# Splitting the third VectorE operation off an activation chain and queueing it one step later, in an eight-core transformer layer

## The chip, the cores and the metric

The kernel runs on the 8 cores of one Trainium2 chip. Each core computes two of the sixteen sequences on its own; nothing is exchanged between cores. The metric is the device time of the slowest core in microseconds (us). Engines are named as in the profile: PE (TensorE), ACT (ScalarE), DVE (VectorE), POOL (GpSimd), SP (SyncE).

## The reference

One pre-norm transformer layer on x of shape 16 x 2048 x 1024, with 16 heads and a feed-forward width of 4096:

```python
x = x + attention(layernorm(x), w_qkv, b_qkv, w_proj, b_proj)
x = x + ffn(layernorm(x), w1, b1, w2, b2)

# ffn: round to multiples of 1/256, piecewise-linear GELU with 33 breakpoints on [-4, 4]
h = float2fix(einsum('bsd,df->bsf', x, w1) + b1, 8)
h = pwlin_gelu_basic(h, 8, 8)       # interp of the exact GELU, 0 below -4, identity above 4
h = float2fix(h, 8)
out = float2fix(einsum('bsf,fd->bsd', h, w2) + b2, 8)
```

## The kernel before

Each engine has a program of its own. The builder walks once through the work and appends closures to one list, each for one engine; an engine executes its own closures in the order in which they were appended. Between engines there are only counting semaphores: `c_v` counts what DVE has finished, `c_s` ACT, `c_pe` PE. `wait_ge(c_v.sem, w)` holds the issuing engine, and all that is queued behind on it, until DVE has counted to `w`.

The first part (layer norm, QKV, attention, projection) writes the intermediate x1s to DRAM. The second part is the feed-forward network, and the change lies in it. It has 8 blocks of 512 tokens (two sequences, four blocks each). A block has 32 groups (`hm`) of 128 hidden channels, and a group is one tile of 128 channels by 512 tokens. The groups of all blocks are numbered through as `h` (0 to 255). A main loop runs over steps `g` (0 to 258). A step appends pieces of four groups, in this order:

- `act_E012(g)`: PE multiplies the eight slices of w1 by xn2 into one of two PSUM halves (L956; the half comes free when ACT has read the group two before); ACT reads it into `ft` (L970, "E1"); DVE clamps and rounds (L981, L984).
- `act_E34(g-1)`: ACT scales into `fu5` (L996); DVE rounds and subtracts (L1004, L1006).
- `act_E56(g-2)`: ACT adds a half (L1022) and takes two GELUs, into `fgl` (L1023) and `fji` (L1025); DVE subtracts them (L1034), multiplies by `fu5` into `fki` (L1036), and adds `fgl` into `fu5` (L1039), with an explicit drain between each two.
- `act_E78(g-3)`: ACT adds the rounding constant (L1055) and writes the finished tile to `gbuf` (L1057). Before L1055 it waits for DVE's L1039 of that group, which was queued one step earlier.

So in a step ACT executes L970, L996, L1022, L1023, L1025, L1055, L1057, and DVE executes L981, L984, L1004, L1006, L1034, L1036, L1039.

Other work is interleaved by `hm`. At `hm` 3, 6, ..., 24 the step begins with 32 matmuls of the second product for the block before (`w2_mm`, L1089); the first of them waits for the last `gbuf` tile of the block before, which L1057 writes at `hm` 2. At `hm` 5, 8, ..., 26 the DVE part of the step begins with three operations that evacuate such a product (`w2_ev`, L1113, L1118, L1120). At `hm` 5, 9, 13, 17 the layer norm of the next block puts, after L981 and L984, two statistics operations and two small ones on DVE, and ACT waits for them before a square root with its table load (`ln2_A`, L862 to L876). At `hm` 6, 10, 14, 18 DVE takes a reciprocal and a product, and ACT waits for them before it normalises a tile (`ln2_B`, L887, L889, L901). After the last step eight `w2_mm` with `w2_ev` follow.

Of the kernel before, what the change touches and what calls it, by code (L numbers as in the profile page):

```python
# [10 lines left out]
ALU = mybir.AluOpType  # L11
# [38 lines left out]
def build():  # L50
# [15 lines left out]
    p = Prog()  # L66
    with es:
# [26 lines left out]
        c_v = Ctr(es, nc, "c_v")  # L94
# [26 lines left out]
        def ev(g):  # L121
            g.dma_start(out=identb[:], in_=ident).then_inc(c_lc.sem, 16)
            g.dma_start(out=bqt[:], in_=bqkv[0:2048].rearrange("(c q) -> q c", q=128),
                        allow_slow_non_contiguous=True).then_inc(c_lc.sem, 16)
            g.dma_start(out=b1t[:], in_=b1.rearrange("(c q) -> q c", q=128),
                        allow_slow_non_contiguous=True).then_inc(c_lc.sem, 16)
            g.dma_start(out=bvbc[:], in_=bqkv[2048:3072].partition_broadcast(128)).then_inc(c_lc.sem, 16)
            g.dma_start(out=bpbc[:], in_=bproj.partition_broadcast(128)).then_inc(c_lc.sem, 16)
            g.dma_start(out=b2bc[:], in_=b2.partition_broadcast(128)).then_inc(c_lc.sem, 16)
# [166 lines left out]
        for s in range(NSEQ):  # L296
# [125 lines left out]
            for g_ in range(4):  # L422
                for mq in range(4):
                    mc = g_ * 4 + mq
                    for tb in range(4):
                        bi = gi % 4
# [35 lines left out]
            for g_ in range(4, 6):  # L462
                nb = g_ - 4
                for tt in range(NTT):
                    bi = gi % 4
# [468 lines left out]
        e1_hist = {}  # L934
        e5_hist = {}
        e6_hist = {}
        e8_hist = {}

        def act_E012(h):
# [50 lines left out]
        def act_E34(h):  # L990
            i = h % 3
            i4 = h % 4

            def ev(sc, i=i, i4=i4, w=e1_hist[(h, "va")]):
                sc.wait_ge(c_v.sem, w)
                sc.activation(fu5[:, i, :], ft[:, i4, :], AF.Identity,  # L996
                              bias=p155[:, 0:1], scale=1.0 / 64.0).then_inc(c_s.sem, 1)
            p.on("scalar", ev)
            c_s.n += 1
            u5_done = c_s.n  # L1000

            def ev(v, i=i, i4=i4, w=u5_done):
                v.wait_ge(c_s.sem, w)
                v.tensor_scalar(fki[:, i4, :], fu5[:, i, :], MC, -MC, ALU.add, ALU.add)  # L1004
                v.drain()  # L1005
                v.scalar_tensor_tensor(ft[:, i4, :], fki[:, i4, :], -1.0, fu5[:, i, :],  # L1006
                                       ALU.mult, ALU.add).then_inc(c_v.sem, 1)
            p.on("vector", ev)
            c_v.n += 1
            e1_hist[(h, "vb")] = c_v.n  # L1010

        def act_E56(h):
            i = h % 3
            i4 = h % 4
            j = h % 2

            def ev(sc, i=i, i4=i4, j=j, w=e1_hist[(h, "vb")], fg=e6_hist.get(h - 2)):
                sc.wait_ge(c_v.sem, w)
                if fg is not None:
                    sc.wait_ge(c_v.sem, fg)  # L1020
                sc.drain()  # L1021
                sc.add(fu5[:, i, :], ft[:, i4, :], phf[:, 0:1])  # L1022
                sc.activation(fgl[:, j, :], fki[:, i4, :], AF.Gelu, bias=neg4[:, 0:1],  # L1023
                              scale=0.25)
                sc.activation(fji[:, j, :], fki[:, i4, :], AF.Gelu, bias=neg375[:, 0:1],  # L1025
                              scale=0.25).then_inc(c_s.sem, 1)
            p.on("scalar", ev)
            c_s.n += 1
            e5_hist[h] = c_s.n
            s3_done = c_s.n  # L1030

            def ev(v, i=i, i4=i4, j=j, w=s3_done):
                v.wait_ge(c_s.sem, w)
                v.tensor_sub(ft[:, i4, :], fji[:, j, :], fgl[:, j, :])  # L1034
                v.drain()  # L1035
                v.scalar_tensor_tensor(fki[:, i4, :], ft[:, i4, :], 256.0, fu5[:, i, :],  # L1036
                                       ALU.mult, ALU.mult)
                v.drain()
                v.scalar_tensor_tensor(fu5[:, i, :], fgl[:, j, :], 256.0, fki[:, i4, :],  # L1039
                                       ALU.mult, ALU.add).then_inc(c_v.sem, 1)  # L1040
            p.on("vector", ev)
            c_v.n += 1
            e6_hist[h] = c_v.n

        def act_E78(h):
            bi, hm = divmod(h, 32)
            i = h % 3
            j = h % 2

            def ev(sc, bi=bi, hm=hm, i=i, j=j, w=e6_hist[h],  # L1050
                   gg=w2_last_of.get(bi - 2)):
                sc.wait_ge(c_v.sem, w)
                if gg is not None:
                    sc.wait_ge(c_pe.sem, gg)
                sc.add(fji[:, j, :], fu5[:, i, :], cmc[:, 0:1])  # L1055
                sc.drain()  # L1056
                sc.activation(gbuf[:, bi % 2, hm, :], fji[:, j, :], AF.Identity,  # L1057
                              bias=nmc256[:, 0:1],
                              scale=1.0 / 256.0).then_inc(c_s.sem, 1)
            p.on("scalar", ev)  # L1060
            c_s.n += 1
            e8_hist[h] = c_s.n
# [3 lines left out]
        def w2_mm(bi, j):  # L1066
            s, tb = blocks[bi]
            tt, nb = j // 2, j % 2
            ob = j % 2
            par = tt % 2  # L1070
            if nb == 0:
                def ev(sy, s=s, tb=tb, tt=tt, par=par, g=x2rd_guard.get(par)):
                    if g is not None:
                        sy.wait_ge(c_v.sem, g)
                    sy.dma_start(out=x1rd2[:, par, :],
                                 in_=x1s[s, tb * TB + tt * 128:tb * TB + (tt + 1) * 128, :]
                                 ).then_inc(s_x[2 + par].sem, 16)
                p.on("sync", ev)
                s_x[2 + par].n += 16

            def ev(t, bi=bi, tt=tt, nb=nb, ob=ob, gd=g_done_of[bi],
                   g=w2ev_guard.get(ob), fw=first_w2[0]):
                if fw:
                    t.wait_ge(c_lb.sem, ldw_B)
                t.wait_ge(c_s.sem, gd)
                if g is not None:
                    t.wait_ge(c_v.sem, g)
                for hm in range(NHM):
                    ins = t.matmul(pA[:, 1024 + ob * 512:1024 + (ob + 1) * 512],  # L1089
                                   gbuf[:, bi % 2, hm, tt * 128:(tt + 1) * 128],  # L1090
                                   w2b[:, hm, nb * 512:(nb + 1) * 512],
                                   start=(hm == 0), stop=(hm == NHM - 1))
                ins.then_inc(c_pe.sem, 1)
            p.on("tensor", ev)
            c_pe.n += 1
            first_w2[0] = False
            w2_pe_of[(bi, j)] = c_pe.n
            w2_last_of[bi] = c_pe.n
# [50 lines left out]
        for g in range(NG + 3):  # L1149
            if g < NG:  # L1150
                bi, hm = divmod(g, NHM)
                if bi > 0 and hm in w2mm_marks:
                    w2_mm(bi - 1, w2mm_marks.index(hm))
                if bi > 0 and hm in w2ev_marks:
                    w2_ev(bi - 1, w2ev_marks.index(hm))
                if hm % 2 == 0 and 2 <= hm // 2 + 1 <= 15:
                    w1_group_load(bi, hm // 2 + 1)
                if hm == 30 and bi + 1 < NB:
                    w1_group_load(bi + 1, 0)
                act_E012(g)  # L1160
                if hm == 31 and bi + 1 < NB:
                    w1_group_load(bi + 1, 1)
                if bi + 1 < NB and 3 <= hm <= 20:
                    tt, st = divmod(hm - 3, 4)
                    if st == 0 and hm >= 3 and tt < 4:
                        ln2_L(bi + 1, tt)
                    elif st == 2:
                        ln2_A(bi + 1, tt)
                    elif st == 3:
                        ln2_B(bi + 1, tt)  # L1170
                    elif st == 1 and tt >= 1:
                        ln2_C1(bi + 1, tt - 1)
                        xn2_ready[bi + 1] = ln2_C2(bi + 1, tt - 1)
            if g >= 1 and g - 1 < NG:
                act_E34(g - 1)
            if g >= 2 and g - 2 < NG:
                act_E56(g - 2)
            if g >= 3 and g - 3 < NG:
                act_E78(g - 3)
                if (g - 3) % NHM == NHM - 1:  # L1180
                    g_done_of[(g - 3) // NHM] = c_s.n
# [58 lines left out]
```

## Time and profile before

| | us |
|---|---|
| time before, median of 2 runs | 3963.19 |
| the two runs | 3918.98 and 4007.39 |
| the profiled execution | 3937.67 |
| its span on the slowest core (core 6) | 3936.1 |
| its spans over the eight cores | 3896.8 to 3936.1 |
| busy of the span: PE, ACT, DVE, POOL | 2680.5, 2506.3, 1969.5, 663.3 |

The span is the time from the first to the last instruction of the core. Busy shares are means over two very different parts: the feed-forward loop begins at about 2296 us and ends at about 3874 us of the span. All rows are of core 6.

### The profile page before, as it was taken

The numbers are of one execution on the slowest core, as the hardware profiler recorded it, in microseconds if no ns is written. First come the engines' busy times: TensorE is split into PE (matmuls) and PEld (weight loads), VectorE is DVE, ScalarE is ACT, GpSimd is POOL, SyncE is SP. The second block draws the span as 40 slices with busy tenths as digits, with TensorE's granted clock in tenths as the row PEclk, the third lists the DMA queues.
The fourth block names the chain that finished last, engine by engine and source line by source line (L and its number), as shares of the span: only waits on it lengthen the run. The fifth ranks groups of instructions, "written<-read, shape, count | busy, mean of one in ns | idle before, by whom it ended". The sixth has DMA issues, their size and how long they took to land.

```text
span 3936.1 us, 41130 instructions; the slowest of 8 cores (3896.8 to 3936.1 us)
## 1 busy us (share of the span) xinstructions
PE 2680.5 (68%) x10880; PEld 939.2 (24%) x10880; DVE 1969.5 (50%) x2865; ACT 2506.3 (64%) x3102; POOL 663.3 (17%) x1234
## 2 busy tenths in 40 slices
PE   0894767677777987776768335676667666766686
PEld 0341211121213421211211111222222222322232
DVE  2013433434341134343434247676777777676794
ACT  0321857767581267585848158787878777787893
POOL 1000000000001100000000223333332333242340
PEclk9986888989898998898989667788878888888898
DMA  8322011010103200101010564344444444354451
GB/s 180 74 28 91 30 41 40 20 44 4 45 4 76 33 2 4 45 4 45 4 44 4 108 96 65 54 78 73 73 72 71 67 78 69 69 80 71 67 90 50
DMA packets 206879, 215.91 MB, mean 55 GB/s; under 512 B 24000, under 2 KB 167360, under 8 KB 206656
## 3 DMA queue, kind: packets, MB, share of 16 engines
q0 software_dynamic: 169792, 95.82, 19.9%
q1 hardware_dynamic: 36864, 117.46, 9.1%
q8 instruction: 99, 1.62, 0.2%
q14 instruction: 124, 1.02, 0.1%
HBM read 265.90 MB, written 33.55 MB: 76 GB/s over the span
## 4 chain that ended last, share of the span: by engine, by line
PE 31%; ACT 19%; DVEq 12%; DVE 11%; ACTq 10%; issue 8%; DMA 7%; POOL 1%; SPq 0%; POOLq 0%
ACT PTb L646 12%; PE pA L442 6%; PE pAT L660 6%; DMA xstream<-x 5%; PE pA L633 5%; ACTq L1056 5%; ACTq L1021 4%; PE pBT L662 4%; DVEq L983 3%; PE pA L479 3%; PE pA L1089 3%; DVE fki L1036 3%; DVEq L1035 3%; ACT fji L1025 2%; DVEq L1005 2%
## 5 line engine op out<-in xcount | busy, mean ns | idle before, releaser
L646 ACT ACTIVATE PTb<-pA,negB 128x1024 bf16<-128x1024 f32 x1024 | 1104.7, 1112 | 460.8 <-PE pA L636 439.2
L956 PE MATMUL pA<-xn,w1s 128*128 128x512 bf16 x2048 | 620.1, 463 | 450.9 <-ACT ft L970 428.1
L819 POOL DMA_DIRECT2D w1s<-w x1024 | 552.6, 585 | 1046.0 <-PE pA L956 1020.9
L660 PE MATMUL pAT<-PTb,vtm 128*65 128x512 bf16 x1024 | 410.3, 401 | 263.7 <-ACT PTb L646 191.5
L1089 PE MATMUL pA<-w2b,gbuf 128*128 128x512 bf16 x2048 | 476.3, 393 | 91.6 <-ACT gbuf L1057 91.6
L633 PE MATMUL pA<-qfm,kfm 64*128 64x512 bf16 x1024 | 406.4, 406 | 42.8 <-DVEq L734 41.5
L956 PEld LDWEIGHTS pA<-xn,w1s 128*128 128x128 bf16 x2048 | 217.0, 111 | 820.5 <-issue 674.9
L662 PE MATMUL pBT<-PTb,vtm 128*65 128x512 bf16 x1024 | 410.1, 401 | 0.0
L636 PE MATMUL pA<-qfm,kfm 64*128 64x512 bf16 x1024 | 406.7, 406 | 0.0
L602 POOL DMA_DIRECT2D attn<-stgB x64 | 33.5, 523 | 1735.6 <-PE pBT L662 1152.6
L1089 PEld LDWEIGHTS pA<-w2b,gbuf 128*128 128x128 bf16 x2048 | 207.5, 102 | 360.0 <-issue 143.0
L442 PE MATMUL pA<-xnfm,wstr 128*128 128x512 bf16 x1024 | 244.7, 407 | 8.8 <-DVEq L734 8.8
L660 PEld LDWEIGHTS pAT<-PTb,vtm 128*65 128x65 bf16 x1024 | 112.6, 110 | 574.2 <-issue 574.2
L518 DVE COPY uAB<-pAT 65x512 f32<-65x512 f32 x64 | 44.0, 687 | 409.2 <-PE pBT L662 409.2
L1034 DVE TENSOR_TENSOR ft<-fji,fgl 128x512 f32<-128x512 f32 x256 | 176.3, 689 | 117.6 <-ACT fji L1025 117.1
L970 ACT ACTIVATE ft<-pA,b 128x512 f32<-128x512 f32 x256 | 171.1, 668 | 100.6 <-PE pA L956 100.6
L530 DVE RECIPROCAL rbsb<-uAB 1x512 bf16<-1x512 f32 x64 | 214.0, 3344 | 11.3 <-issue 9.3
L538 DVE RECIPROCAL rbsb<-uAB 1x512 bf16<-1x512 f32 x64 | 210.2, 3285 | 0.0
L492 DVE TENSOR_TENSOR vtm<-pA,bvbc 128x512 bf16<-128x512 f32 x64 | 44.4, 694 | 323.6 <-PE pA L479 323.6
L633 PEld LDWEIGHTS pA<-qfm,kfm 64*128 64x128 bf16 x1024 | 91.0, 93 | 470.9 <-issue 469.6
L1022 ACT ACTIVATE fu<-ft,phf 128x512 f32<-128x512 f32 x256 | 184.9, 722 | 23.7 <-DVE ft L1006 2.6
L1057 ACT ACTIVATE gbuf<-fji,nmc 128x512 bf16<-128x512 f32 x256 | 184.8, 722 | 18.4 <-issue 1.0
(79 smaller groups left out, 3269.9 us busy)
## 6 DMA issues: line engine op xcount, KB each, us to landing
w1s<-w POOLq DMA_DIRECT2D x1024, 64.0 KB, 2.7
xstream<-x SPq DMA_DIRECT2D x96, 512.0 KB, 4.0
x1rd<-x1s SPq DMA_DIRECT2D x64, 512.0 KB, 4.5
x1s<-x1t SPq DMA_DIRECT2D x32, 512.0 KB, 2.9
out<-outt SPq DMA_DIRECT2D x64, 256.0 KB, 2.3
wstr<-wqkv POOLq DMA_DIRECT2D x96, 128.0 KB, 6.1
w2b<-w POOLq DMA_DIRECT2D x32, 256.0 KB, 26.7
attn<-stgB POOLq DMA_DIRECT2D x64, 64.0 KB, 1.9
```

What stands on the lines that cost most here:

```text
L442: ins = t.matmul(psl[bi], wstr[:, g_ % 2, dc, mq * 128:(mq + 1) * 128], xnfm[:, dc, tb * 512:(tb + 1) * 512], start=(dc == 0), stop=(dc == ...
L530: v.reciprocal(rbsb[64:65, 0:512], uAB[64:65, 0, :]).then_inc(c_v.sem, 1)
L538: v.reciprocal(rbsb[64:65, 512:1024], uAB[64:65, 1, :]).then_inc(c_v.sem, 1)
L633: t.matmul(pA[:, off:off + 512], kfm[0:64, pr, ko:ko + 128], qfm[0:64, pr, qs:qs + 512], start=True, stop=True, skip_group_check=True)
L636: t.matmul(pA[:, off + 512:off + 1024], kfm[64:128, pr, ko:ko + 128], qfm[64:128, pr, qs:qs + 512], start=True, stop=True, skip_group_chec ...
L646: sc.activation(PT[:, kt % 2, :], pA[:, off:off + 1024], AF.Exp, bias=negB[:, 0:1], scale=SCALE).then_inc(c_s.sem, 1)
L660: t.matmul(pAT[0:65, :], lhs[:, 2 * pr, :], PT[:, kt % 2, 0:512], start=(kt == 0), stop=(kt == NKT - 1), skip_group_check=True)
L662: t.matmul(pBT[0:65, :], lhs[:, 2 * pr + 1, :], PT[:, kt % 2, 512:1024], start=(kt == 0), stop=(kt == NKT - 1), skip_group_check=True).the ...
L819: gp.dma_start(out=w1s[:, sl, dc, :], in_=w1[dc * 128:(dc + 1) * 128, grp * 256:(grp + 1) * 256]).then_inc(c_lw[sl].sem, 16)
L956: ins = t.matmul(pA[:, hb * 512:(hb + 1) * 512], w1s[:, sl, dc, (hm % 2) * 128:(hm % 2 + 1) * 128], xn2[:, bi % 2, dc, :], start=(dc == 0) ...
L1056: sc.drain()
L1089: ins = t.matmul(pA[:, 1024 + ob * 512:1024 + (ob + 1) * 512], gbuf[:, bi % 2, hm, tt * 128:(tt + 1) * 128], w2b[:, hm, nb * 512:(nb + 1) ...
```

## The change

The DVE closure of `act_E56` is cut after its second operation, which now counts `c_v`. The third operation becomes a function of its own, `act_E6b(h)`, called one step later, between `act_E56(g-2)` and `act_E78(g-3)`. `act_E78` now waits for the count of `act_E6b`. The explicit drain that stood before the third operation is gone; in its place stands a wait on `c_v` for the second operation. ACT's L996 gets a further wait, for `act_E6b` three groups before. The two waits on `e6_hist` (before L970 and before L1022) keep their names and now refer to the second operation.

```diff
@@ act_E34 @@
-            def ev(sc, i=i, i4=i4, w=e1_hist[(h, "va")]):
+            def ev(sc, i=i, i4=i4, w=e1_hist[(h, "va")], vd=e6b_hist.get(h - 3)):
                 sc.wait_ge(c_v.sem, w)
+                if vd is not None:
+                    sc.wait_ge(c_v.sem, vd)
@@ act_E56 @@
                 v.scalar_tensor_tensor(fki[:, i4, :], ft[:, i4, :], 256.0, fu5[:, i, :],
-                                       ALU.mult, ALU.mult)
-                v.drain()
+                                       ALU.mult, ALU.mult).then_inc(c_v.sem, 1)
+            p.on("vector", ev)
+            c_v.n += 1
+            e6_hist[h] = c_v.n
+
+        def act_E6b(h):
+            i = h % 3
+            i4 = h % 4
+            j = h % 2
+
+            def ev(v, i=i, i4=i4, j=j, w=e6_hist[h]):
+                v.wait_ge(c_v.sem, w)
                 v.scalar_tensor_tensor(fu5[:, i, :], fgl[:, j, :], 256.0, fki[:, i4, :],
                                        ALU.mult, ALU.add).then_inc(c_v.sem, 1)
             p.on("vector", ev)
             c_v.n += 1
-            e6_hist[h] = c_v.n
+            e6b_hist[h] = c_v.n
@@ act_E78 @@
-            def ev(sc, bi=bi, hm=hm, i=i, j=j, w=e6_hist[h],
+            def ev(sc, bi=bi, hm=hm, i=i, j=j, w=e6b_hist[h],
@@ main loop @@
             if g >= 2 and g - 2 < NG:
                 act_E56(g - 2)
             if g >= 3 and g - 3 < NG:
+                act_E6b(g - 3)
                 act_E78(g - 3)
```

## Rows read from the trace of the kernel before

**Rows 1.** The page, part 1: busy us, share of the span, instructions.
```profile
PE 2680.5 (68%) x10880; PEld 939.2 (24%) x10880; DVE 1969.5 (50%) x2865; ACT 2506.3 (64%) x3102; POOL 663.3 (17%) x1234
```

**Rows 2.** Windows: before the feed-forward loop, the loop, and behind it.
```profile
core 6: us, PE busy (x) PEld busy (x) DVE busy (x) ACT busy (x) POOL busy (x), PEclk, DMA share, GB/s
...
2296.00:3874.00 1578.00, 1036.44 (x4048) 415.18 (x4046) 1159.63 (x2155) 1262.87 (x1904) 543.81 (x1008) 0.81 0.45 71
```

**Rows 3.** Waits from 2300 to 3900 us: total, times, longest.
```profile
ACT L876 <- DVE ln2d L867: 130.4, 28, 5.3
...
ACT ft L970 <- PE pA L956: 76.6, 8, 11.0
...
ACT xn2tm L901 <- DVE ln2d L889: 60.6, 28, 3.6
...
ACT fu L1022 <- DVE ft L1006: 2.6, 8, 0.5
ACT fji L1055 <- DVE fu L1039: 1.9, 3, 1.1
```

**Rows 4.** Timeline, ACT, one step: start us, duration us, operation.
```profile
2891.07 0.71 ACT L1025 ACTIVATE fji<-fki,neg 128x512 f32<-128x512 f32 x1
2891.68 0.71 ACT L1055 ACTIVATE fji<-fu,cmc 128x512 f32<-128x512 f32 x1
...
2893.09 0.67 ACT L970 ACTIVATE ft<-pA,b 128x512 f32<-128x512 f32 x1
...
2895.69 0.71 ACT L1025 ACTIVATE fji<-fki,neg 128x512 f32<-128x512 f32 x1
```

**Rows 5.** Timeline, DVE, the same step.
```profile
2891.88 0.69 DVE L1034 TENSOR_TENSOR ft<-fji,fgl 128x512 f32<-128x512 f32 x1 [0.45 <-ACT fji L1025]
2892.65 0.69 DVE L1036 SCALAR_TENSOR_TENSOR fki<-ft,fu 128x512 f32<-128x512 f32 x1
2893.41 0.69 DVE L1039 SCALAR_TENSOR_TENSOR fu<-fgl,fki 128x512 f32<-128x512 f32 x1
2894.02 0.42 DVE L981 TENSOR_SCALAR fki<-ft 128x512 f32<-128x512 f32 x1
...
2894.86 0.42 DVE L1004 TENSOR_SCALAR fki<-fu 128x512 f32<-128x512 f32 x1
2895.36 0.69 DVE L1006 SCALAR_TENSOR_TENSOR ft<-fki,fu 128x512 f32<-128x512 f32 x1
```

**Rows 6.** Timeline, both engines, the last step of the loop.
```profile
3869.69 0.71 ACT L1025 ACTIVATE fji<-fki,neg 128x512 f32<-128x512 f32 x1
...
3872.03 0.69 DVE L1039 SCALAR_TENSOR_TENSOR fu<-fgl,fki 128x512 f32<-128x512 f32 x1
3872.87 0.72 ACT L1055 ACTIVATE fji<-fu,cmc 128x512 f32<-128x512 f32 x1 [1.08 <-DVE fu L1039]
```

**Rows 7.** Timeline: ACT and DVE where E1 ended a long wait (`hm` 3).
```profile
2908.68 0.69 ACT L970 ACTIVATE ft<-pA,b 128x512 f32<-128x512 f32 x1 [10.89 <-PE pA L956]
...
2909.55 0.43 DVE L981 TENSOR_SCALAR fki<-ft 128x512 f32<-128x512 f32 x1 [10.82 <-ACT ft L970]
```

**Rows 8.** Timeline, layer-norm steps `hm` 6 and 9: DVE's L981, ACT's release.
```profile
2931.29 0.42 DVE L981 TENSOR_SCALAR fki<-ft 128x512 f32<-128x512 f32 x1
...
2932.77 1.24 ACT L901 ACTIVATE xn2tm<-x1rd,ln2d 128x1024 bf16<-128x1024 f32 x1 [1.75 <-DVE ln2d L889]
...
2950.06 0.42 DVE L981 TENSOR_SCALAR fki<-ft 128x512 f32<-128x512 f32 x1
...
2952.82 1.28 ACT L876 ACT_TABLE_LOAD   x1 [4.95 <-DVE ln2d L867]
```

**Rows 9.** Timeline, PE: matmuls of both products.
```profile
2898.05 8.76 PE L1089 MATMUL pA<-w2b,gbuf 128*128 128x512 bf16 x32 [9.94 <-ACT gbuf L1057]
...
3020.52 3.57 PE L956 MATMUL pA<-xn,w1s 128*128 128x512 bf16 x8 [6.96 <-ACT ft L970]
...
3056.65 1.89 PE L956 MATMUL pA<-xn,w1s 128*128 128x512 bf16 x8 [3.43 <-ACT ft L970]
```

More of the change, by code:

```diff
@@ L936, in build @@
         e6_hist = {}
+        e6b_hist = {}
         e8_hist = {}
```

## The prediction, made before the changed kernel ran

> **What bounds the kernel now.** The page's busy shares come first: ACT is busy for 64% of the span [rows 1]. This is a mean over unlike parts, so the windows come next. The feed-forward loop, in which the whole change lies, takes 1578 us, and in it ACT is busy for 1262.9 us, DVE for 1159.6 us and PE for 1036.4 us, with PE's granted clock at 0.81 of full speed, between its two levels of 1.2 and 2.4 GHz [rows 2]. What stands before and behind the loop is the same code in both kernels.
>
> The timeline of one step then shows how the two elementwise engines stand to each other. ACT goes from one L1025 to the next in 2895.69 - 2891.07 = 4.62 us and is never idle in it [rows 4]. DVE runs the same group one step behind and has 0.45 us to spare in the step [rows 5]. The important thing to see is that L1055 starts 0.61 us after L1025 [rows 4], while DVE has only just begun L1034 [rows 5]: ACT doesn't look at this step's DVE work, because L1055 waits for an L1039 that was queued a step before. That one step of slack is why the waits list has only 1.9 us, in 3 places, for ACT's L1055 on DVE's L1039 [rows 3]. The real waits of ACT in the loop are the layer norm's (130.4 us at L876, 60.6 us at L901) and PE at the block starts (76.6 us at L970) [rows 3]. So ACT sets the pace of ordinary steps, and DVE that of the layer-norm steps.
>
> **The change part by part.**
>
> *The moved operation and the wait for it.* In step g, DVE's queue now reads L981 and L984 of group g, L1004 and L1006 of g-1, L1034 and L1036 of g-2, and only then the third operation of g-3. Its own inputs have long been there. But it stands behind L1034 of g-2, which needs L1025 of g-2, which ACT executes directly before L1055 of g-3. And L1055 now waits for the third operation. The slack of a step is gone: in every step ACT must stand still from the end of its second GELU until DVE has done three operations.
>
> How long that is, counted from the start of L1025: L1034 starts 2891.88 - 2891.07 = 0.81 us later; L1036 0.77 us after that [rows 4, 5]; the third operation, which has no drain ahead of it any more, 0.61 us after that, as L981 follows L1039 without a drain (2894.02 - 2893.41) [rows 5]. It starts at 2.19 us. From the start of such an operation to a waiting L1055 the last step of the loop shows 3872.87 - 3872.03 = 0.84 us [rows 6]. So L1055 starts 3.03 us after L1025. The same last step is the case in small: there ACT had no slack, and L1055 started 3872.87 - 3869.69 = 3.18 us after L1025, with the drain still in it [rows 6]. Before, the distance was 0.61 us [rows 4]. An ordinary step becomes 3.03 - 0.61 = 2.42 us longer, 7.04 us for 4.62.
>
> Queued behind the waiting L1055 on ACT are L1057, then L970 of the next group, for which PE (its PSUM half) and DVE (L981) wait in turn.
>
> *How many.* There are 256 groups. For 255 the price is 2.42 us: 617.1 us. For the last one the operation has been queued right behind the one of the group before, and is done by the time ACT gets there; in place of 3.18 - 0.61 = 2.57 us ACT spends there the 1.40 us of L1055 and L1057 (L1055 to L970 is 2893.09 - 2891.68 = 1.41 us [rows 4]): -1.2 us.
>
> *What is given back.* In a layer-norm step ACT waits behind L970 for a DVE chain. Now DVE is no longer behind when L970 ends, so this wait shrinks. L981 starts 2909.55 - 2908.68 = 0.87 us after the start of an L970 that it waited for [rows 7], that is 0.20 us after its end (0.67 us long [rows 4]). From L981 the table load of L876 starts 2952.82 - 2950.06 = 2.76 us later, and L901 2932.77 - 2931.29 = 1.48 us later [rows 8]. New waits: 0.20 + 2.76 = 2.96 us and 0.20 + 1.48 = 1.68 us. The 28 old ones of each kind sum to 130.4 and 60.6 us [rows 3]; given back are 130.4 - 28 x 2.96 = 47.5 us and 60.6 - 28 x 1.68 = 13.6 us. The evacuation of a second product at the head of a step, 1.9 us of DVE (an estimate from three spacings like those of [rows 5]: 0.77, 0.50 and 0.61 us), then falls into the 2.5 us in which DVE waits for the next L970 (from 2.80 to 5.31 us after L1025: 3.03 + 1.41 + 0.87), and costs nothing. The small waits for a lagging DVE go too: 2.6 us at L1022 and 1.9 - 1.1 us at L1055 [rows 3], 3.4 us together.
>
> *What stays.* The block-start wait of 10.89 us [rows 7] runs from L1057 at `hm` 2 through 32 second-product matmuls and 8 first-product ones to L970. Both ends move together, so none of it is given back. PE elsewhere stays hidden: between two marks it has three groups and one second product, at most 3 x 3.57 + 8.76 = 19.5 us [rows 9], against three steps of 21.1 us. DVE's own step: L1004 comes 0.84 us after L981 [rows 5], L1006 0.50 us after that and lasts 0.69 us [rows 5], so it ends by 5.31 + 0.84 + 0.50 + 0.69 = 7.34 us, before the next L1034 is released at 7.04 + 0.81 = 7.85 us, and DVE doesn't become a second bound. The copy of a transposed tile, one more DVE operation in four steps of a block, takes 0.61 us of spacing (taken as that of [rows 5]) and overshoots by 0.1 us at most.
>
> *Waits themselves.* The further wait of ACT before L996 has been satisfied for a step. Its price is between 0 and what the drain costs on DVE, 0.16 us (0.77 - 0.61 [rows 5]), times 253 = 40 us. I take 0: L970, with two waits already, follows at the pace of its neighbours. The dropped drain lies on the new path, so a third operation that followed at 0.77 us would cost 255 x 0.16 = 41 us more. I take 0.61 us, as the row with a satisfied wait has it.
>
> On this point the Trainium skill says otherwise (VectorE: DVE Perf Modes, The DRAIN you can't avoid): a next operation doesn't start before the pipe is empty, and leaving semaphores out saves nothing. In this trace a 0.69 us operation is followed after 0.61 us where no drain stands. By the page the sum would be about 41 us higher, by the rows it is not.
>
> *Sum.* 617.1 - 1.2 - 47.5 - 13.6 - 3.4 = 551.4 us, say 550. On the profiled execution's own 3937.67 us that gives 4488 us, 14% more. The profiled execution lies between the two runs (3918.98 and 4007.39) and 25 us under their median, so the forecast holds for an execution like it; one like the longer run would be some 70 us higher.
>
> **The rivals.**
>
> *PE turns cold and becomes the bound.* PE's gaps grow by 2.4 us a step. Eight first-product matmuls took 3.57 us at the slow level and 1.89 us at the fast one [rows 9]. If all ran slow, a second product would take 4 x 3.57 = 14.3 us, and PE would need 10.7 + 14.3 = 25.0 us for three steps of 21.1: 7 marks in each of 7 blocks at 3.9 us give 191 us, and seven block starts (14.3 - 8.76) + (3.57 - 1.89) = 7.2 us each give 50 us: 4729 us. Against it: a second product that followed 9.94 us of idleness took only 8.76 us [rows 9], so a run of matmuls gets the fast clock back in its course. The Trainium skill (TensorE: Matmul & The Clock Gate, Part 1) has the same two levels, set by how busy the array has lately been, which is the rule that speaks for this rival. Chance 5%.
>
> *The stall is mostly taken out of waits that exist already.* If the block-start waits shrank to nothing, 76.6 us more would come back: 4411 us. It needs PE to start before L1057 of `hm` 2, which the wait forbids. With the unknown on the other small terms, 4%.
>
> *It makes no difference.* It would need ACT to reach L1055 at least 3.03 us after L1025 anyway, for some other reason. Nothing stands between them on ACT. Then 3938 us, 2%.
>
> *Faster: DVE sets the pace, and the shorter chain speeds it up.* If DVE were the bound, every step would save the drain's 0.16 us: 256 x 0.16 = 41 us, 3897 us. It decides where DVE has no idle time in a step and ACT has; the rows show 0.45 us of idle time on DVE [rows 5] and ACT full. It holds only in a few steps behind evacuations. Chance 1%.
>
> **How the numbers follow.** The forecast, the stall in every step, has 88%, and its time is 4488 us. Its own unknowns are 41 us upward for the drain, up to 40 us for the wait, some 20 us down (the given-back terms and the faster run), and the 70 us of a longer execution. That makes 4445 to 4585 us, and what lies outside it (rivals and the tails) is under 2 in 10. A measurement of this kernel can tell about 2% from no change; faster 1%, within 2% 2%, slower 97%.
>
> **What would show it.** In the profile after: a wait of ACT's L1055 on the third DVE operation some 250 times, near 2.3 us each and 590 us in total; L1055 starting 3.0 us after L1025 (3.2 if the drain's cost stays); an ordinary step of 7.04 us; mean waits of 3.0 us at L876 and 1.7 us at L901; L970 still waiting about 10.9 us once a block; DVE's busy time unchanged, its idle time ahead of L981 in every step; the attention part unchanged. If PE's L956 appeared as what L970 waits for at the marks, the first rival would hold. The forecast is wrong if L1055 still starts 0.6 us after L1025.

## The result, and the profile after

| | before | after |
|---|---|---|
| all runs, median, us | 3967.75 (3916.35 to 4018.16, 10 runs) | 4522.95 (4464.50 to 4562.53, 11 runs) |
| profiled execution, us | 3937.67 | 4464.50 |
| span of core 6 | 3936.1 | 4455.8 |
| span of core 1 | 3914.4 | 4463.0 |
| feed-forward loop, first E1 to the start of the last `gbuf` write, core 6 | 1579.3 | 2132.5 |
| the same, core 1 | 1583.5 | 2130.2 |

In some executions of any of these kernels the cores of one half of the chip, or of both, show a lower granted clock and take some per cent longer, so ratios and single times below are of executions without that (experiment 3, which has none, is read on the cores that were spared), while the medians of the table are of all. The change makes the kernel slower: the ratio is 1.146, with a 95% interval of 1.138 to 1.155. The loop is the number to compare, since it is the part that was changed: it grew by 553.2 us on core 6 and by 546.7 us on core 1.

Waits inside the loop, after (core 1, the slowest one): engine and line, what it waited for, us in total, times, longest.

```profile
PE pA L957 <- ACT ft L971: 816.5, 186, 11.3
DVE fki L982 <- ACT ft L971: 600.9, 254, 18.4
ACT fji L1068 <- DVE fu L1052: 588.9, 254, 2.7
...
ACT ft L971 <- PE pA L957: 99.6, 10, 19.7
ACT L876 <- DVE ln2d L867: 83.7, 28, 3.3
ACT xn2tm L901 <- DVE ln2d L889: 46.6, 28, 1.7
```

(E1, L970 of before, is L971 here; DVE's L981 is L982; the second GELU, L1025, is L1028; DVE's subtraction, multiplication and third operation, L1034, L1036 and L1039, are L1037, L1039 and L1052; ACT's add, L1055, is L1068. For PE, L956 is L957 and L1089 is L1102.) Where ACT's add waited 1.9 us in 3 places before [rows 3], it waits 588.9 us in 254 places now. In exchange DVE waits 600.9 us for ACT's next E1, in 254 places (97.1 us in 9 places on this core before): the two engines take turns. The layer-norm waits shrank from 130.4 and 60.6 us [rows 3, core 6] to 83.7 and 46.6 us, which are the totals of core 6 after as well.

An ordinary step after, ACT and then DVE, to be laid beside [rows 4, 5]:

```profile
3256.75 0.71 ACT L1028 ACTIVATE fji<-fki,neg 128x512 f32<-128x512 f32 x1
3259.77 0.72 ACT L1068 ACTIVATE fji<-fu,cmc 128x512 f32<-128x512 f32 x1 [2.31 <-DVE fu L1052]
...
3263.79 0.71 ACT L1028 ACTIVATE fji<-fki,neg 128x512 f32<-128x512 f32 x1
```

```profile
3257.56 0.69 DVE L1037 TENSOR_TENSOR ft<-fji,fgl 128x512 f32<-128x512 f32 x1 [0.54 <-ACT fji L1028]
3258.32 0.69 DVE L1039 SCALAR_TENSOR_TENSOR fki<-ft,fu 128x512 f32<-128x512 f32 x1
3258.93 0.69 DVE L1052 SCALAR_TENSOR_TENSOR fu<-fgl,fki 128x512 f32<-128x512 f32 x1
3262.03 0.48 DVE L982 TENSOR_SCALAR fki<-ft 128x512 f32<-128x512 f32 x1 [2.41 <-ACT ft L971]
```

The chain is plain to see: second GELU at 3256.75, DVE's subtraction 0.81 us later, the multiplication, the third operation of the older group (0.61 us behind it), and 0.84 us after its start ACT's add. From GELU to add it is 3.02 us (0.61 before), and from GELU to GELU 7.04 us (4.62 before).

The window of the loop after, on core 6 as [rows 2] for before (length, then busy us of PE, PEld, DVE, ACT and POOL with counts, granted clock, DMA share, GB/s):

```profile
2261.00:4394.00 2133.00, 1165.57 (x4056) 443.13 (x4054) 1166.20 (x2156) 1289.64 (x1905) 543.43 (x1008) 0.73 0.33 52
```

DVE does the same work (1166.2 us for 1159.6 us [rows 2]), and so, but for 2%, does ACT (1289.6 for 1262.9 us). The 2% are overlap that was lost: before, the add started 0.61 us after a GELU that lasts 0.71 us [rows 4], and the wait ends this overlap of 0.10 us in every step, some 26 us in 255 steps (an estimate). PE looks busier, 1165.6 for 1036.4 us, with no instruction more: its granted clock fell from 0.81 to 0.73, and it idles longer between groups. The page's slices show the clock as well, 40 of them over the span, in tenths of full speed; first those of before (core 6), then those of after (core 1):

```profile
PEclk9986888989898998898989667788878888888898
```

```profile
PEclk9989888889899988989666687786868767676887
```

### The profile page after: what moved, and what is told of

Its sections match the earlier page's. It is cut to its first block, busy times and chain, and to the rows that moved or that the text cites. A ratio compares the mean times of both kernels' runs of the same rounds, so it can differ in the third digit from the quotient of the medians.

```text
span 4463.0 us, 41383 instructions; the slowest of 8 cores (4444.6 to 4463.0 us)
## 1 busy us (share of the span) xinstructions
PE 2763.3 (62%) x10880; PEld 953.5 (21%) x10880; DVE 1978.9 (44%) x2865; ACT 2530.8 (57%) x3102; POOL 661.3 (15%) x1234
## 4 chain that ended last, share of the span: by engine, by line
ACT 30%; PE 27%; DVE 13%; issue 11%; ACTq 7%; DMA 7%; DVEq 5%; POOL 1%; SPq 0%; POOLq 0%
ACT PTb L646 10%; ACTq L1024 6%; PE pAT L660 5%; PE pA L442 5%; DMA xstream<-x 5%; PE pA L633 5%; ACT fji L1068 4%; DVE ft L1037 4%; ACT fu L1025 4%; PE pBT L662 3%; ACT fgl L1026 3%; ACT fji L1028 3%; DVE fu L1052 3%; PE pA L1102 3%; PE pA L479 2%
## 5 line engine op out<-in xcount | busy, mean ns | idle before, releaser
L957 PE MATMUL pA<-xn,w1s 128*128 128x512 bf16 x2048 | 733.8, 525 | 835.3 <-ACT ft L971 816.5
L1102 PE MATMUL pA<-w2b,gbuf 128*128 128x512 bf16 x2048 | 483.2, 397 | 152.0 <-ACT gbuf L1070 152.0
L1068 ACT ACTIVATE fji<-fu,cmc 128x512 f32<-128x512 f32 x256 | 184.7, 721 | 591.2 <-DVE fu L1052 588.9
L957 PEld LDWEIGHTS pA<-xn,w1s 128*128 128x128 bf16 x2048 | 236.4, 122 | 1297.8 <-issue 1210.7
L982 DVE TENSOR_SCALAR fki<-ft 128x512 f32<-128x512 f32 x256 | 112.2, 438 | 600.9 <-ACT ft L971 600.9
L1102 PEld LDWEIGHTS pA<-w2b,gbuf 128*128 128x128 bf16 x2048 | 208.9, 103 | 427.0 <-issue 214.7
L1037 DVE TENSOR_TENSOR ft<-fji,fgl 128x512 f32<-128x512 f32 x256 | 177.1, 692 | 171.9 <-ACT fji L1028 171.7
L442 PE MATMUL pA<-xnfm,wstr 128*128 128x512 bf16 x1024 | 226.2, 385 | 9.7 <-DVEq L734 9.7
L971 ACT ACTIVATE ft<-pA,b 128x512 f32<-128x512 f32 x256 | 171.2, 669 | 99.6 <-PE pA L957 99.6
L1025 ACT ACTIVATE fu<-ft,phf 128x512 f32<-128x512 f32 x256 | 184.9, 722 | 21.8 <-issue 1.1
```

The source lines that it names most:

```text
L442: ins = t.matmul(psl[bi], wstr[:, g_ % 2, dc, mq * 128:(mq + 1) * 128], xnfm[:, dc, tb * 512:(tb + 1) * 512], start=(dc == 0), stop=(dc == ...
L957: ins = t.matmul(pA[:, hb * 512:(hb + 1) * 512], w1s[:, sl, dc, (hm % 2) * 128:(hm % 2 + 1) * 128], xn2[:, bi % 2, dc, :], start=(dc == 0) ...
```

## The experiments

Each loop length is given as above, from the first E1 to the start of the last `gbuf` write, on cores 0 and 1: 1579.6 and 1583.5 us before, 2131.5 and 2130.2 us in the changed kernel.

**1. The same split, the operation queued early (e1_early).**

```diff
+            if g >= 3 and g - 3 < NG:
+                act_E6b(g - 3)
             if g >= 1 and g - 1 < NG:
                 act_E34(g - 1)
...
             if g >= 3 and g - 3 < NG:
-                act_E6b(g - 3)
                 act_E78(g - 3)
```

> The changed kernel with one call moved: act_E6b(g-3) is called right behind act_E012(g), ahead of act_E34(g-1), so DVE executes it before this step's L1034. The split, the semaphore in place of the drain and all waits stay. Theory of the place (ACT's add waits for an operation that is queued behind work which needs the GELU directly ahead of that add): the wait goes, the add starts 0.61 us after the second GELU again, the feed-forward loop (first E1 to the last gbuf write, 1579 us before and 2130 us in the changed kernel) takes 1565 to 1590 us, and the time is that of before within 1%. Rival, cost of the split itself (one more semaphore, two more waits): the loop stays near 2130 us. Rival, PE's clock (the first product's matmul took 525 ns in the mean, 463 before): nothing about PE is changed by moving a DVE operation, so the time stays near that of the changed kernel unless the gaps close.

Measured: the ratio to before is 1.0004, interval 0.9961 to 1.0047, and the loop takes 1568.8 us (core 0) and 1569.4 us (core 1). The step of the new kernel, core 0:

```profile
3260.59 0.70 ACT L1028 ACTIVATE fji<-fki,neg 128x512 f32<-128x512 f32 x1
...
3261.20 0.71 ACT L1068 ACTIVATE fji<-fu,cmc 128x512 f32<-128x512 f32 x1
...
3265.20 0.71 ACT L1028 ACTIVATE fji<-fki,neg 128x512 f32<-128x512 f32 x1
```

The add is back at 0.61 us, the step at 4.61 us. All semaphores and waits of the change are still there, so splitting by itself costs nothing that shows in the time. One call, placed two calls later in the step, costs the 550 us. The loop is even 11 us (core 0) and 14 us (core 1) shorter than before, which is too little to show in the whole time. It is a balance: on core 0 ACT's waits at L876 and L901 fell from 130.4 to 101.9 and from 60.6 to 53.8 us, and the add still waits for the moved operation 37 times, 25.5 us in total (1.9 us before).

**2. Only the wait, nothing split or moved (e2_wait_only).**

```diff
 # the kernel before, act_E78
-            def ev(sc, bi=bi, hm=hm, i=i, j=j, w=e6_hist[h],
+            def ev(sc, bi=bi, hm=hm, i=i, j=j, w=e6_hist.get(h + 1, e6_hist[h]),
```

> The kernel before with nothing but the wait of act_E78(h) changed: it waits for the third DVE operation of group h+1 instead of h. Nothing is split or moved. Theory of the place: this wait alone makes the loss, with the drain still in the chain: the add starts 3.18 us after the second GELU, an ordinary step takes 4.62 + 2.57 = 7.19 us, and with 61 us given back in the layer-norm waits the loop takes 1579 + 655 - 64 = 2170 us, 40 us more than in the changed kernel; time about 4530 us. Rival, cost of the split: nothing is split, so 3940 us.

Measured: 4502 us in one execution, the loop 2172.3 us (core 0) and 2173.8 us (core 1), for 2170 expected. The waits of core 1:

```profile
ACT fji L1055 <- DVE fu L1039: 623.7, 251, 3.3
```

The kernel before, told to wait for one DVE group too many, loses as much as the changed kernel and 41 to 44 us more, for the drain that is still in its chain (run 4 tests that part by itself).

**3. The third operation between the two others (e3_mid).**

```diff
                 v.tensor_sub(ft[:, i4, :], fji[:, j, :], fgl[:, j, :])
-                v.drain()
+            p.on("vector", ev)
+            if h >= 1:
+                act_E6b(h - 1)
+
+            def ev(v, i=i, i4=i4, j=j):
+                v.drain()
```

> The changed kernel with the third operation of the group before queued between this step's subtraction and multiplication, in the place of the drain. Theory of the place: the price goes by how many GELU-dependent operations stand ahead of it. It starts 0.81 + 0.61 = 1.42 us after the second GELU, the add 0.84 us later at 2.26 us, the step takes 4.62 + 1.65 = 6.27 us, and the loop 1579 + 255 x 1.65 - 64 = 1936 us; time about 4290 us. Rival, cost of the split: unchanged at 2130 us. Rival, PE's clock: no proportion to the place.

Measured: the loop takes 1941.7 us on core 0 and on core 1, for 1936 expected. The three executions took 4388, 4403 and 4407 us; in the profiled one (4388 us) the spans of cores 0 to 3 are 4259 to 4273 us, for the 4290 us expected. The wait of core 0 and a step of it (the add is L1073 here, the third operation L1057):

```profile
ACT fji L1073 <- DVE fu L1057: 388.3, 249, 2.0
```

```profile
3261.95 0.71 ACT L1028 ACTIVATE fji<-fki,neg 128x512 f32<-128x512 f32 x1
...
3268.23 0.71 ACT L1028 ACTIVATE fji<-fki,neg 128x512 f32<-128x512 f32 x1
3269.04 0.69 DVE L1037 TENSOR_TENSOR ft<-fji,fgl 128x512 f32<-128x512 f32 x1 [0.52 <-ACT fji L1028]
3269.64 0.69 DVE L1057 SCALAR_TENSOR_TENSOR fu<-fgl,fki 128x512 f32<-128x512 f32 x1
...
3270.48 0.72 ACT L1073 ACTIVATE fji<-fu,cmc 128x512 f32<-128x512 f32 x1 [1.55 <-DVE fu L1057]
```

GELU to add is 2.25 us, and GELU to GELU 6.28 us. With the operation ahead of the GELU-dependent ones the price is next to nothing, behind one of them 1.64 us a step, behind two 2.41 us: it goes by the place in the queue, operation by operation.

**4. The drain put back (e4_drain).**

```diff
                 v.wait_ge(c_v.sem, w)
+                v.drain()
                 v.scalar_tensor_tensor(fu5[:, i, :], fgl[:, j, :], 256.0, fki[:, i4, :],
```

> The changed kernel with an explicit drain put back ahead of the moved third operation. Measures the term on which the prediction chose between two values. If the rows are right (0.61 us from start to start without a drain, 0.77 us with one), the add starts 3.18 us after the second GELU for 3.02 us, and the loop grows from 2130 to about 2171 us, as in e2_wait_only (2173 us). If a vector operation empties its pipe in any case, the drain costs nothing and the loop stays at 2130 us.

Measured: 4512 us in the only execution, the loop 2178.7 us (core 0) and 2176.7 us (core 1), 47 us more than the changed kernel's 2131.5 and 2130.2 us. A step of core 7, the slowest one (the add is L1069, the third operation L1053):

```profile
3264.20 0.71 ACT L1028 ACTIVATE fji<-fki,neg 128x512 f32<-128x512 f32 x1
...
3265.78 0.69 DVE L1039 SCALAR_TENSOR_TENSOR fki<-ft,fu 128x512 f32<-128x512 f32 x1
3266.56 0.69 DVE L1053 SCALAR_TENSOR_TENSOR fu<-fgl,fki 128x512 f32<-128x512 f32 x1
...
3267.41 0.72 ACT L1069 ACTIVATE fji<-fu,cmc 128x512 f32<-128x512 f32 x1 [2.49 <-DVE fu L1053]
```

From the multiplication to the third operation it is 0.78 us with the drain and 0.61 us without, and from GELU to add 3.21 us (3.18 expected). So the drain costs 0.17 us where the chain is exposed, of which 255 places make 43 of the 47 us, and the prediction's choice of 0.61 us was right.

**5. The lesson turned round: the layer-norm waits (f1_ln, f5_ln_early).** Before the change ACT already waited 191 us in the same manner, for layer-norm operations queued on DVE just ahead of the instruction that needs them. The DVE part and the ACT part were taken apart in the kernel before: `ln2_As` and `ln2_Bs` keep ACT's square root and ACT's normalisation at their old steps, and `ln2_A` and `ln2_B` are left with DVE's operations, a step earlier.

```diff
                     elif st == 2:
-                        ln2_A(bi + 1, tt)
+                        ln2_As(bi + 1, tt)
                     elif st == 3:
-                        ln2_B(bi + 1, tt)
+                        ln2_Bs(bi + 1, tt)
...
             if g >= 2 and g - 2 < NG:
                 act_E56(g - 2)
+            if g < NG and bi + 1 < NB and 4 <= hm <= 17:
+                if hm % 4 == 0:
+                    ln2_A(bi + 1, (hm - 4) // 4)
+                elif hm % 4 == 1:
+                    ln2_B(bi + 1, (hm - 5) // 4)
```

> The kernel before with the same lesson applied the other way, to the layer-norm waits: the DVE part of ln2_A is queued at the end of the step before its square root, and the DVE part of ln2_B at the end of the step before its normalisation, so ACT finds both done. Theory: the 191 us that ACT waits at L876 and L901 mostly go. But DVE is then near its own limit (per block about 163 us of DVE issue against 164 us of ACT), so not all is won: time 3938 - 120 = 3820 us, 3750 to 3880. Rival (DVE already sets the pace of these blocks): the waits reappear at L1022 or L1055 and the time stays within 1%.

Measured: 3831 and 3833 us, beside 3903 us and more for the kernel before on the same chip; the loop 1497.4 us (core 0) and 1500.6 us (core 1), against 1579.6 and 1583.5 us before: 82 us less, for the 120 expected. The waits show why it was short (core 2; L876 and L901 are L879 and L907 here):

```profile
ACT L879 <- DVE ln2d L867: 82.9, 28, 4.2
...
ACT xn2tm L907 <- DVE ln2d L892: 25.5, 28, 1.3
```

The statistics stood behind the three operations L1034, L1036 and L1039 of before, which need the GELU. The next kernel has the five added lines ahead of `act_E56(g - 2)` and is otherwise the same.

> f1_ln with the DVE parts of ln2_A and ln2_B queued ahead of that step's L1034 instead of behind L1039. In f1_ln ACT still waited 83 us at L876 and 26 us at L901, because the statistics stood behind three operations that need the GELU, the very thing that the change of this case did to its third operation. Theory: both waits fall under 20 us in total, the loop goes from 1500 to about 1420 us, time 3740 to 3790 us. Rival (DVE sets the pace): the waits reappear at L1022 and L1055 and the time stays near f1_ln's 3831 us.

Measured: 3741 and 3745 us; the loop 1415.4 and 1417.7 us. The waits left are just over the 20 us expected (core 5):

```profile
ACT L879 <- DVE ln2d L867: 22.9, 20, 2.0
```

Moving the same operations from behind `act_E56` to ahead of it gained another 82 us, and the wait at L907 is gone from the list. That is the change of this case, run backwards, at another place. DVE doesn't set the pace: ACT's waits at L1028 and L1061 (L1022 and L1055 of before) stayed at 2.3 and 1.5 us (core 5; 2.6 and 1.9 us before [rows 3]).

**6. Later marks, and both together (f2_marks, f6_ln_marks).**

```diff
-        w2mm_marks = (3, 6, 9, 12, 15, 18, 21, 24)
-        w2ev_marks = (5, 8, 11, 14, 17, 20, 23, 26)
+        w2mm_marks = (5, 8, 11, 14, 17, 20, 23, 26)
+        w2ev_marks = (7, 10, 13, 16, 19, 22, 25, 28)
```

> The kernel before with the second product's matmuls at hm 5, 8, ..., 26 for 3, 6, ..., 24 and their evacuations two steps later than before too. ACT's block-start wait (10.9 us, seven times) is taken by PE executing 32 matmuls ahead of the first product of hm 3. With two finished halves in PSUM ACT has 9.2 us of work meanwhile: the wait falls to 1 to 3 us, the loop by 7 x 9 = 60 us, time about 3865 us. Rival: PE becomes late at a later mark and the wait only moves.

Measured: 3825 us in the profiled execution, the loop 1500.5 and 1501.1 us, 79 and 82 us less for the 60 expected. ACT's wait for PE, 99.1 us in 10 places before (core 1, the start of the loop included), fell to 28.3 us in 8 places on core 1; on core 3, the slowest one, it is

```profile
ACT ft L970 <- PE pA L956: 31.2, 9, 20.3
```

where 20.3 us are the one wait at the start of the loop. The layer-norm waits fell a little with it (118.2 us at L876 on core 3), which is part of what came beyond the 60 us.

> Both: the early layer-norm parts and the later marks. If the two waits are independent, the gains add: loop about 1360 us, time 3680 to 3740 us. If DVE or PE has no room left, less than the sum.

Measured: ratio to before 0.937, interval 0.931 to 0.943, 3666 to 3679 us; the loop 1345.6 and 1343.3 us, 15 us under the expected 1360. The waits that are left on core 1:

```profile
ACT ft L976 <- PE pA L962: 27.8, 6, 21.2
...
ACT L879 <- DVE ln2d L867: 22.6, 17, 2.1
```

The gains nearly add: 164 and 79 us (core 0) make 243 us, and 234 us came. This kernel is faster than both kernels of the case.

## Why the prediction was right, step by step

*Who sets the pace.* That ACT had a full step of slack towards DVE, and that the change takes exactly this, was the step that carried all the rest. Runs 1 and 2 show it from both sides: the moved operation without the place costs nothing, the wait without the moved operation costs all of it.

*The price of a step.* Predicted 3.03 us from GELU to add and a step of 7.04 us; measured 3.02 and 7.04 us. The four pieces (0.81, 0.77, 0.61 and 0.84 us) all came from rows of before, and the row of the last step, where ACT had no slack, set 3.18 us beside their sum, with the drain in it. Run 4 shows that case at 3.21 us. The 41 us that the prediction has "by the page" were a reading of half a section: The DRAIN you can't avoid, in the Trainium skill's VectorE: DVE Perf Modes, also says that a next operation that is not held starts earlier. So the page didn't call for 41 us more, and the 0.61 us of the rows agree with that sentence.

*The count.* 254 waits of 588.9 us in total, on core 1, for "some 250 times, near 2.3 us each and 590 us". Core 6 has 255 of 590.9 us, and on core 1 one more of 2.3 us is put down to PE. The last add starts 1.41 us after the one before it (4397.10 and 4398.51 us on core 1), without a wait, as the term of -1.2 us had it.

*What is given back.* New mean waits of 83.7 / 28 = 2.99 us and 46.6 / 28 = 1.66 us, for 2.96 and 1.68 us.

*What stays.* The block-start wait was not given back. One of them in the changed kernel, on core 1, reads

```profile
3364.46 0.69 ACT L971 ACTIVATE ft<-pA,b 128x512 f32<-128x512 f32 x1 [11.41 <-PE pA L957]
```

for the 10.89 us of before [rows 7]. PE had idled 17.07 us ahead of it, for 9.94 us before [rows 9], and took 9.29 us for the 32 matmuls, for 8.76 us.

```profile
3353.29 9.29 PE L1102 MATMUL pA<-w2b,gbuf 128*128 128x512 bf16 x32 [17.07 <-ACT gbuf L1070]
```

The seven block-start waits sum to 80.3 us on core 6 (75.8 before) and to 78.4 us on core 1 (77.2 before), while single ones ran from 10.6 to 11.9 us on core 1 already before. So the true part of the rival of the cold PE is at most some 5 us. The rest of it didn't come: in the loop ACT waited for PE at L971 only 10 times, 99.6 us with the three waits at the start of the loop, as on the same core before (99.1 us, 10 times). The granted clock fell to 0.73, and E1 waited for PE no more often than before.

*The sum.* Predicted for the loop, +551 us; measured +553.2 us on core 6 and +546.7 us on core 1. Most of the difference between the two cores lies in the loop of before, which is 4.2 us longer on core 1. The forecast of the whole time, 4488 us, stands between the profiled 4464.5 us and the median of 4523 us, and the range of 4445 to 4585 us holds all runs. What is off against the profiled execution, 23.5 us, doesn't lie in the change: the sum was added to an execution whose slowest core reached the loop at 2294.4 us; the same core reached it at 2261.0 us in the execution after. This first part is the same code in both. It came with a granted clock of 0.87 before and 0.90 after on this core, and PE busy for 1585.2 and 1530.6 us in it; why PE is granted more in one execution stays open. So the whole time was forecast less well than the loop, and the range, which allowed for a longer execution, had room for it.

*The rivals "no difference" and "faster"* are out by the loop, 550 us longer, and by the 588.9 us of waits. The cost of the extra wait ahead of L996 was taken as 0: run 1 has that wait, and its loop is no longer than before.

## What to carry to other kernels

In a software pipeline over engines with in-order queues, look not at when an operation's inputs are ready but at what is queued ahead of it: an operation whose result another engine needs next belongs ahead of the operations that wait for that engine's newest output. The price can be read off before anything is built: in every step it is the distance from the newest output to the end of the queued chain, less what the waiting engine would have spent anyway (3.03 less 0.61 us here). And where a wait of this form is already in the list of waits, the opposite move is worth trying: in this kernel two moves of layer-norm operations and one of matmuls took 6% off the kernel.

## What the runs showed of the hardware

Two things stand out. The spacings of an ordinary step hold to 0.01 us from kernel to kernel (0.81, 0.77, 0.61 and 0.84 us in the kernel before, and 0.81, 0.76, 0.61 and 0.84 us in the one after), so that a loop of 2130 us could be worked out to 5 us from a dozen rows. Not every step is an ordinary one: on core 1 of the changed kernel GELU to add is 3.01 or 3.02 us in 174 of 256 steps and 2.96 or 2.97 us in 54. And a vector operation of 0.69 us was followed by the next after 0.61 us without a drain and after 0.78 us with one; the loop with the drain in its 255 exposed places was 47 us longer. So the explicit drain has a price here where another engine waits for what stands behind it; no run takes one out elsewhere.
